# One-token shift ahead of the feed-forward norm: three SBUF-to-SBUF transfers in place of three matmuls

## The chip, the cores and the metric

One core of a Trainium2 chip runs the whole program. The metric is the device time of one execution in microseconds (us).

## What is computed

The input `x` is 16 sequences of 256 tokens of 256 channels. A first block adds cross attention over a short context. The second block works on the normed result: two layers of local attention and a gated feed-forward part. Attention is local, in windows of 128 tokens that also see the window before. A layer is, shortened:

```
h = shift_token(x)                 # second half of the channels: from the token before
q, k, v = split(h @ wqkv)          # l2norm, scale, rotary
x = x + local_attention(q, k, v) @ wo
h = shift_token(x)                 # <- this shift is what is changed
h = (h - mean(h)) / sqrt(var(h) + 1e-5) * lg + lb
a, g = split(h @ w1 + b1)
x = x + (a * gelu(g)) @ w2 + b2
```

`shift_token` keeps channels 0 to 127 and takes channels 128 to 255 from the token before (zeros at the first token).

## The kernel before, in words

All matmuls with weights are made of three products of a high and a low part. The program has a phase for the cross attention (up to about 300 us) and then the layer phase, with which the change deals. There 32 items (2 layers of 16 sequences) go through a software pipeline. Iteration `g` works on four items at once: `a = g` (projection to q, k, v, rotation, turning), `b = g - 1` (scores, softmax, values, output product, first residual), `c = g - 2` (shift, norm, first feed-forward product, gate) and `d = g - 3` (second feed-forward product, second residual). A tile holds a sequence as 2 tiles of 128 tokens on the partitions.

Each engine has its own program in a fixed order written by hand, in a function `run_l(g)`; the engines meet by semaphores. What a step waits for stands in its helper.

- The first residual (VectorE, line 1302) writes `x1[:, :, 0:3:2]`: of the three slots of 128 channels, slot 0 gets the first half and slot 2 the second. Slot 1 is for the second half shifted by one token. Semaphore `dve_x1`.
- TensorE's `shift_down(c)` (lines 678 to 683) waits for `dve_x1` and multiplies slot 2 by a shifted identity: one matmul for tile 0, one for tile 1, and one that brings the last row of tile 0 to the first row of tile 1. It stands between `project(a, d, 0, 1)` and `project(a, d, 0, 0)`. VectorE's `copy_shifted(c)` (line 1307) copies the result to slot 1, and `stats_h(c)` (line 1312) follows, then `rotate(a, 0)` (lines 1350, 1356).
- TensorE's order after that: `feed(c, d, 0)` to `feed(c, d, 5)` (line 788) between projections and scores, `turn_p(..., 0)` (line 748), `turn_h`, `turn_p` 1 and 2, `turn_next` (line 520, transposes of `x_cur` for the next item), `weigh` (line 764), `hidden` 0 to 2, `turn_p(..., 5)`, `weigh`, `hidden` 3 to 5, `out_product`, `turn_qk` (line 826).
- `maxes` (VectorE, line 1371) finds the maxima of a unit of scores; the fifth waits for `turn_p(..., 0)`. `second_residual(d)` (line 1409) waits for the last `feed`, and in layer 2 adds the block's input to it (line 1414). Semaphores `dve_x2` and `dve_out`.
- SyncE issues all transfers, in this order in an iteration: the tail copies (lines 455 and 459: 42 rows of the last chunk of the gated values, copied to further partitions in SBUF, used by `feed(..., 5)`); the load of `x_cur` for item `a + 1` (line 476, needed by `turn_next` of the same iteration, after the wait that the old content has been read); after the wait for `dve_x1` the load of `x_res` for `b` (line 480); after the wait for `dve_x2` or `dve_out` the store of `x2` (line 488); and from item 16 on for `c` the load of `x_orig` (line 490).

Of the kernel before, what the change touches and what calls it, by code (L numbers as in the profile page):

```python
# [25 lines left out]
P = 128  # L26
SEQS, T, D = 16, 256, 256
NT = T // P
# [20 lines left out]
XUNITS = 4  # L49


WEIGHT = {name: n + 1 for n, name in enumerate(
# [26 lines left out]

def identities():  # L80

    return np.eye(P, 2 * P + 4, k=4, dtype=np.float32)


def at(n, per, k):


    if isinstance(n, int):
        return n * per + k
    i, c = n  # L90
    return i * (2 * per) + (c * per + k)
# [20 lines left out]
def build(nc, x, ctx_in, xwq, xwk, xwv, xwo, xbo, wqkv, qsc, ksc, wo, lng, lnb, w1, b1, w2, b2, rope, mask, ident, out):  # L112
    ctx = ExitStack()
    with ctx:
        def sb(name, shape, dt=F32, where=ctx):
            return where.enter_context(nc.sbuf_tensor(name, shape, dt))

        def sem(name):
            return ctx.enter_context(nc.semaphore(name))
# [5 lines left out]
        pb = ctx.enter_context(nc.psum_tensor("pb", [P, 8, 512], F32))  # L125
        ones_at = sb("ones_at", [P, 2 * P + 4])
        id_f, down_f, carry_f = ones_at[:, 4:4 + P], ones_at[:, 3:3 + P], ones_at[:, 3 + P:3 + 2 * P]
        mask_t = sb("mask_t", [P, 2, P])
# [125 lines left out]
            "cur_load", "res_load", "orig_load", "x2_store")]  # L254
        pe_down, dve_down = sem("pe_down"), sem("dve_down")
        pe_xt, act_xhi, dve_xlo = sem("pe_xt"), sem("act_xhi"), sem("dve_xlo")
# [62 lines left out]
        def has_next(a):  # L319
            return a is not None and not (isinstance(a, int) and a == ITEMS - 1)  # L320
# [30 lines left out]
        def _(sp):  # L351
# [111 lines left out]
            sp.wait_ge(y_store, 16 * SEQS)  # L463

            def run_l(g, layer=None):
                a, b, c, d, par = l_roles(g)
                if isinstance(d, int) and d == SEQS:
                    tail_weights(1)
                if isinstance(d, int) and d == 0:
                    sp.wait_ge(zero_made, 2)  # L470
                if d is not None:
                    tail_hi(d)
                    tail_lo(d)
                if has_next(a):
                    sp.wait_ge(pe_xt, at(a, 1, 1))
                    sp.dma_start(x_cur[:], one(y_dram, seq_of(plus(a, 1), layer))).then_inc(cur_load, 16)
                if c is not None:
                    sp.wait_ge(dve_x1, at(c, 1, 1))
                    if b is not None:
                        sp.dma_start(x_res[:], one(y_dram, seq_of(b, layer))).then_inc(res_load, 16)  # L480
                if d is not None:
                    if layer_of(d, layer) == LAYERS - 1:
                        sp.wait_ge(dve_out, at(plus(d, -SEQS), 1, 1))
                        dst = out_rows
                    else:
                        sp.wait_ge(dve_x2, at(d, 1, 1))
                        dst = y_dram
                    sp.dma_start(one(dst, seq_of(d, layer)), x2[:, 1 - par]).then_inc(x2_store, 16)
                    if c is not None and layer_of(c, layer) == LAYERS - 1:
                        sp.dma_start(x_orig[:], one(x1_dram, seq_of(c, layer))).then_inc(orig_load, 16)  # L490

            def between(g):
# [10 lines left out]
        def _(pe):  # L503
# [173 lines left out]

            def shift_down(c):

                pe.wait_ge(dve_x1, at(c, 1, 1))  # L680
                pe.matmul(pb[:, 6, 0:P], down_f, x1[:, 0, 2], start=True, stop=True)
                pe.matmul(pb[:, 6, P:2 * P], down_f, x1[:, 1, 2], start=True, stop=False)
                pe.matmul(pb[:, 6, P:2 * P], carry_f, x1[:, 0, 2], start=False, stop=True).then_inc(pe_down, 1)

            def turn_h(b, c):
# [65 lines left out]
            def weigh(b, c, par, j):  # L751

                pe.wait_ge(act_pt, at(b, UNITS, 2 * j + 2))
                if j == 0:
                    pe.wait_ge(act_v, at(b, NT, NT))
                    if c is not None:
                        pe.wait_ge(dve_down, at(c, 1, 1))
                for k in range(2 if j < 2 else 4):
# [71 lines left out]
            def run_l(g, layer=None):  # L830
# [3 lines left out]
                if a is not None:  # L834
                    project(a, d, 0, 1)
                if c is not None:
                    shift_down(c)
                if a is not None:
# [321 lines left out]
        def _(dve):  # L1160
# [143 lines left out]

            def copy_shifted(c):
                dve.wait_ge(pe_down, at(c, 1, 1))
                nc.vector.tensor_copy(x1[:, :, 1], pb[:, 6, 0:2 * P].rearrange("p (t n) -> p t n", t=NT)).then_inc(dve_down, 1)

            def stats_h(c):
                dve.wait_ge(dve_down, at(c, 1, 1))  # L1310
                for t in range(NT):
                    e = nc.vector.bn_stats(l_st[:, t], x1[:, t, 0:2].rearrange("p c n -> p (c n)"))
                e.then_inc(dve_bst, 1)
                aggregate(l_mv, l_st, dve_bst, dve_bmv, c)
# [107 lines left out]
            def run_l(g, layer=None):  # L1422
# [7 lines left out]
                if c is not None:  # L1430
                    copy_shifted(c)
                    stats_h(c)
# [83 lines left out]
        def _(pool):  # L1516
# [38 lines left out]


            nc.gpsimd.memset(hg_hi[:, FC - 1].bitcast(F32), 0.0).then_inc(zero_made, 1)

# [104 lines left out]
```

## Time and profile before

| | |
|---|---|
| median of 3 runs | 1534.05 us (1534.04 to 1535.44) |
| profiled execution, its own time | 1534.95 us |
| its span, first to last instruction | 1533.1 us |
| TensorE matmuls busy | 1447.2 us (94%) |
| VectorE busy | 1129.9 us (74%) |
| ScalarE busy | 937.8 us (61%) |
| GpSimd busy | 746.9 us (49%) |
| mean granted TensorE clock | 0.98 of full speed |
| share of 16 DMA engines, the queue of all transfers | 11.7% |

The profile shows one execution. PE is TensorE's matmuls, PEld its weight loads, DVE VectorE, ACT ScalarE, POOL GpSimd, and SPq SyncE's sequencer, which issues transfers. Times are us from the start of the span; L520 is line 520. A chain is followed backwards from the last instruction, at each step to what released it. The name behind `<-` in brackets is what ended the idle time before an instruction. The ends of matmuls are modelled, so neighbours overlap in the rows. The granted clock is given as a share of 2.4 GHz: 1.00, or 0.50 for 1.2 GHz.

### The profile page before, as it was taken

Reading aid. Unit: us, or ns where it says so; the run is one execution under the profiler, and the core shown is the slowest. Engines: PE = TensorE matmul, PEld = TensorE weight load, DVE = VectorE, ACT = ScalarE, POOL = GpSimd, SP = SyncE. Lnnn points to the kernel's source line nnn. Section 1 sums busy time; section 2 is a strip of 40 time slices with the busy share of each in tenths; the row PEclk is TensorE's granted clock in tenths of the full one; section 3 lists DMA queues with packets and bytes.
Section 4 is the critical chain, followed back from the end, with each engine's and each line's share of the span. In section 5 each row is a group of like instructions: output and inputs, shape, how many; then the busy total and the mean of one; then the engine's idle time right before and its main releaser. Section 6 shows DMA issues by size and latency. Waiting matters only on the chain.

```text
span 1533.1 us, 33616 instructions
## 1 busy us (share of the span) xinstructions
PE 1447.2 (94%) x11808; PEld 1278.1 (83%) x11808; DVE 1129.9 (74%) x3102; ACT 937.8 (61%) x2670; POOL 746.9 (49%) x570
## 2 busy tenths in 40 slices
PE   4999999868999999999999899999999999999987
PEld 4888888746888888888888788888888888888886
DVE  3766666446788877877777778888788888888874
ACT  2766666435666666666666666666666666666661
POOL 1121121044666666665655555555555655555642
PEclk8999999889999999999999999999999999999999
DMA  6311111200000000000001010011110100001100
GB/s 195 102 55 49 51 54 41 84 29 15 24 24 24 24 24 23 23 23 23 24 26 35 16 56 24 30 39 40 31 31 31 30 30 30 30 30 33 34 24 26
DMA packets 40843, 58.88 MB, mean 38 GB/s; under 512 B 6540, under 2 KB 22448, under 8 KB 40752
## 3 DMA queue, kind: packets, MB, share of 16 engines
q1 hardware_dynamic: 40752, 57.69, 11.7%
q8 instruction: 54, 0.88, 0.2%
q14 instruction: 37, 0.30, 0.1%
HBM read 38.06 MB, written 16.78 MB: 36 GB/s over the span
## 4 chain that ended last, share of the span: by engine, by line
PE 66%; DVE 18%; issue 7%; ACT 4%; POOL 2%; SPq 1%; DMA 1%; DVEq 0%; POOLq 0%; ACTq 0%
PE pb L511 26%; PE pb L788 7%; PE pb L733 6%; PE pb L802 6%; PE pb L764 4%; PE pb L826 4%; DVE p_t L1371 3%; DVE p_t L1385 3%; PE pb L748 3%; DVE r_cos L1350 2%; DVE n_sq L1336 2%; PE pb L572 2%; DVE r_sin L1356 2%; PE pb L560 2%; PE pb L610 2%
## 5 line engine op out<-in xcount | busy, mean ns | idle before, releaser
L1561 POOL TENSOR_TENSOR n_inv<-n_cl,half_neg 128x16 f32<-128x16 f32 x64 | 211.2, 3300 | 199.3 <-DVE n_cl L1341 195.9
L1058 ACT ACTIVATE p_t<-p_t,s_nm 128x128 f32<-128x128 f32 (+1 forms) x512 | 226.6, 444 | 34.5 <-DVE s_nm L1371 31.8
L511 PE MATMUL pb<-h_hi,w_hi 128*128 128x256 f32 x704 | 208.7, 296 | 5.7 <-DVE h_lo L1332 3.3
L511 PE MATMUL pb<-h_hi,w_lo 128*128 128x256 f32 x704 | 199.6, 284 | 0.0
L511 PE MATMUL pb<-h_lo,w_hi 128*128 128x256 f32 x704 | 199.4, 283 | 0.0
L1566 POOL TENSOR_TENSOR r_cos<-r_cos,r_sin 128x1024 f32<-128x1024 f32 x64 | 154.7, 2418 | 89.6 <-DVE r_sin L1356 89.6
L1371 DVE CUSTOM_DVE_ANT_0 p_t<-pb,mask_t 128x128 f32<-128x128 f32 (+1 forms) x512 | 152.0, 353 | 46.3 <-PE pb L733 30.4
L1016 ACT ACTIVATE qk_sq<-pb 128x512 f32<-128x512 f32 x128 | 72.3, 591 | 184.5 <-PE pb L511 184.5
L1049 ACT ACTIVATE pt_t<-pb 128x512 f32<-128x512 f32 x192 | 113.7, 593 | 100.5 <-PE pb L748 100.4
L511 PE MATMUL pb<-wqkv_hi,xt_hi 128*128 128x512 f32 x384 | 166.5, 434 | 5.8 <-DVE r_sin L1356 4.9
L1588 POOL TENSOR_TENSOR hg_lo<-hg,hg_hi 128x256 fp32r<-128x256 f32 x192 | 139.6, 748 | 53.9 <-DVE hg_hi L1402 53.9
L511 PE MATMUL pb<-wqkv_lo,xt_hi 128*128 128x512 f32 x384 | 152.4, 397 | 0.0
L511 PE MATMUL pb<-wqkv_hi,xt_lo 128*128 128x512 f32 x384 | 151.9, 396 | 0.0
L511 PEld LDWEIGHTS pb<-h_hi,w_hi 128*128 128x128 f32 x704 | 134.8, 191 | 17.6 <-issue 6.7
L511 PEld LDWEIGHTS pb<-h_lo,w_hi 128*128 128x128 f32 x704 | 135.3, 192 | 0.0
L511 PEld LDWEIGHTS pb<-h_hi,w_lo 128*128 128x128 f32 x704 | 134.9, 192 | 0.0
L1385 DVE TENSOR_TENSOR p_t<-p_t,s_inv 128x512 f32<-128x512 f32 x192 | 129.4, 688 | 0.1
L748 PE MATMUL pb<-ones_at,p_t 128*128 128x128 f32 x768 | 115.1, 279 | 12.4 <-DVE p_t L1385 11.8
L1573 POOL TENSOR_TENSOR r_cos<-r_cos,n_inv 128x1024 f32<-128x1024 f32 x64 | 122.0, 1906 | 5.0
L1527 POOL TENSOR_TENSOR x_ve<-x_mv,eps_t 128x2 f32<-128x2 f32 x32 | 6.3, 197 | 237.7 <-DVE x_mv L1171 237.0
L733 PE MATMUL pb<-qk_t 64*128 64x128 f32 (+1 forms) x1024 | 111.7, 348 | 5.2 <-DVE wqkv_lo L1164 4.0
L748 PEld LDWEIGHTS pb<-ones_at,p_t 128*128 128x128 f32 x768 | 84.8, 140 | 32.9 <-DVE p_t L1385 19.3
(137 smaller groups left out, 4083.9 us busy)
## 6 DMA issues: line engine op xcount, KB each, us to landing
x_cur<-y_state SPq DMA_DIRECT2D x32, 256.0 KB, 2.7
x_res<-y_state SPq DMA_DIRECT2D x32, 256.0 KB, 2.9
x_in<-x SPq DMA_DIRECT2D x16, 256.0 KB, 2.8
x_state<-x_x SPq DMA_DIRECT2D x16, 256.0 KB, 2.0
y_state<-y_x SPq DMA_DIRECT2D x16, 256.0 KB, 2.1
y_state<-x SPq DMA_DIRECT2D x16, 256.0 KB, 2.0
x_orig<-x_state SPq DMA_DIRECT2D x16, 256.0 KB, 2.8
out<-x SPq DMA_DIRECT2D x16, 256.0 KB, 2.2
```

The costliest lines, as they stand in the source:

```text
L511: mm = pe.matmul(dst, s, m, start=(n == 0 and k == 0), stop=(n == len(pairs) - 1 and k == 2))
L733: mm = pe.matmul(pb[:, S_BANK[u], k * keys:k * keys + keys], qk_t[r:r + DH, 0, ch, q_cols], qk_t[r:r + DH, 1, ch, 0:keys], start=True, sto ...
L748: mm = pe.transpose(pb[:, PT_BANK[u], k * P:k * P + P], p_t[:, u % 4, k * P:k * P + P], id_f)
L788: mm = pe.matmul(pb[:, 7, t * D:t * D + D], s[:, k, rows], m[:, k], start=(k == 0 and j == 0 and t == 0), stop=(k == FC - 1 and t == NT - 1))
L1049: nc.scalar.activation(pt_t[:, u % 4], pb[:, PT_BANK[u]], ACT.Copy).then_inc(act_pt, 1)
L1058: e = nc.scalar.activation(pu, pu, ACT.Exp, bias=s_nm[:, j, k:k + 1], scale=-1.0, accum_out=s_sum[:, j, k:k + 1])
L1371: e = nc.vector.tensor_tensor_reduce(p_t[:, j % 4, k * keys:k * keys + keys], pb[:, S_BANK[j], k * keys:k * keys + keys], m, -1.0, FAR, AL ...
L1385: nc.vector.tensor_tensor(pu, pu, s_inv[:, u, 0:heads].unsqueeze(2).broadcast_to([P, heads, 512 // heads]), ALU.mult).then_inc(dve_pn, 1)
L1561: nc.gpsimd.tensor_tensor(n_inv[:, t], n_cl[:, t], half_neg[:], ALU.pow).then_inc(pool_inv, 1)
L1566: nc.gpsimd.tensor_tensor(r_cos[:, t], r_cos[:, t], r_sin[:, t], ALU.add).then_inc(pool_sum, 1)
L1573: nc.gpsimd.tensor_tensor(rows, rows, n_inv[:, t].unsqueeze(2).broadcast_to([P, 2 * HEADS, DH]), ALU.mult).then_inc(pool_qk, 1)
L1588: nc.gpsimd.tensor_tensor(hg_lo[0:rows, m], hg[0:rows, m], hg_hi[0:rows, m].bitcast(F32), ALU.subtract).then_inc(pool_hglo, 1)
```

## The change

- The three matmuls and the copy are gone, with the shifted parts of the identity constant. Three transfers within SBUF, issued by SyncE, write slot 1 of `x1` from slot 2: rows 0 to 111 to rows 1 to 112 of both tiles, rows 112 to 126 to rows 113 to 127 of both tiles, and row 127 of tile 0 to row 0 of tile 1. The zero row is set once, by GpSimd.
- `stats_h(c)` on VectorE waits for all three.
- SyncE's order in an iteration is now: wait for `dve_x1`, the three shifts, the load of `x_res`; the tail copies; the wait for `dve_x2` or `dve_out`, the store of `x2`, the load of `x_orig`; the load of `x_cur`.
- `weigh(..., 0)` on TensorE, which writes where the shift's result lay, waits for `dve_x1` in place of the copy.

```diff
+SHIFT_PIECES = [(0, 112), (112, 15)]
...
-        pe_down, dve_down = sem("pe_down"), sem("dve_down")
+        shift_load = sem("shift_load")
...
+            def shift_down(c):
+
+                for first, rows in SHIFT_PIECES:
+                    sp.dma_start(x1[first + 1:first + 1 + rows, :, 1], x1[first:first + rows, :, 2]).then_inc(shift_load, 16)
+                sp.dma_start(x1[0:1, 1, 1], x1[P - 1:P, 0, 2]).then_inc(shift_load, 16)
...
-                if isinstance(d, int) and d == 0:
+                if isinstance(g, int) and g == 2:
                     sp.wait_ge(zero_made, 2)
+                if c is not None:
+                    sp.wait_ge(dve_x1, at(c, 1, 1))
+                    shift_down(c)
+                    if b is not None:
+                        sp.dma_start(x_res[:], one(y_dram, seq_of(b, layer))).then_inc(res_load, 16)
                 if d is not None:
                     tail_hi(d)
                     tail_lo(d)
-                if has_next(a):
-                    sp.wait_ge(pe_xt, at(a, 1, 1))
-                    sp.dma_start(x_cur[:], one(y_dram, seq_of(plus(a, 1), layer))).then_inc(cur_load, 16)
-                if c is not None:
-                    sp.wait_ge(dve_x1, at(c, 1, 1))
-                    if b is not None:
-                        sp.dma_start(x_res[:], one(y_dram, seq_of(b, layer))).then_inc(res_load, 16)
-                if d is not None:
                     if layer_of(d, layer) == LAYERS - 1:
                         sp.wait_ge(dve_out, at(plus(d, -SEQS), 1, 1))
...
+                if has_next(a):
+                    sp.wait_ge(pe_xt, at(a, 1, 1))
+                    sp.dma_start(x_cur[:], one(y_dram, seq_of(plus(a, 1), layer))).then_inc(cur_load, 16)
...
-            def shift_down(c):
-
-                pe.wait_ge(dve_x1, at(c, 1, 1))
-                pe.matmul(pb[:, 6, 0:P], down_f, x1[:, 0, 2], start=True, stop=True)
-                pe.matmul(pb[:, 6, P:2 * P], down_f, x1[:, 1, 2], start=True, stop=False)
-                pe.matmul(pb[:, 6, P:2 * P], carry_f, x1[:, 0, 2], start=False, stop=True).then_inc(pe_down, 1)
...
                     if c is not None:
-                        pe.wait_ge(dve_down, at(c, 1, 1))
+                        pe.wait_ge(dve_x1, at(c, 1, 1))
...
-                if c is not None:
-                    shift_down(c)
...
-            def copy_shifted(c):
-                dve.wait_ge(pe_down, at(c, 1, 1))
-                nc.vector.tensor_copy(x1[:, :, 1], pb[:, 6, 0:2 * P].rearrange("p (t n) -> p t n", t=NT)).then_inc(dve_down, 1)
-
             def stats_h(c):
-                dve.wait_ge(dve_down, at(c, 1, 1))
+                dve.wait_ge(shift_load, at(c, 48, 48))
...
+            nc.gpsimd.memset(x1[:, 0, 1], 0.0)
             nc.gpsimd.memset(hg_hi[:, FC - 1].bitcast(F32), 0.0).then_inc(zero_made, 1)
```

## Rows read from the trace of the kernel before

**Rows 1.** The profile's page: TensorE's busy time, and the chain's shares by engine.
```profile
PE 1447.2 (94%) x11808; PEld 1278.1 (83%) x11808; DVE 1129.9 (74%) x3102; ACT 937.8 (61%) x2670; POOL 746.9 (49%) x570
...
PE 66%; DVE 18%; issue 7%; ACT 4%; POOL 2%; SPq 1%; DMA 1%; DVEq 0%; POOLq 0%; ACTq 0%
```

**Rows 2.** Chain in order of time, layer 1: start us, us, engine, line, count.
```profile
645.46 0.66 PE pb L748 x4
...
659.03 0.22 PE pb L681 x2
...
681.91 0.66 PE pb L748 x4
```

**Rows 3.** Chain in order of time, layer 2.
```profile
1167.82 0.66 PE pb L748 x4
...
1204.73 0.66 PE pb L748 x4
```

**Rows 4.** TensorE timeline, layer 1: start us, us, engine, line, op [idle before].
```profile
671.58 0.39 PE L788 MATMUL pb<-w_hi,hg_hi 128*128 128x256 f32 x2
...
674.53 0.60 PE L520 MATMUL pb<-ones_at,x_cur 128*128 128x128 f32 x4
...
681.91 0.66 PE L748 MATMUL pb<-ones_at,p_t 128*128 128x128 f32 x4 [0.22 <-DVE p_t L1385]
```

**Rows 5.** VectorE timeline, layer 1.
```profile
656.57 0.69 DVE L1302 TENSOR_TENSOR x<-pb,x_res 128x512 f32<-128x512 f32 x1 [1.18 <-PE pb L802]
...
660.20 0.75 DVE L1312 BATCH_NORM_STATS2 l_st<-x 128x6 f32<-128x256 f32 x2
...
662.32 1.29 DVE L1350 TENSOR_TENSOR r_cos<-pb,cos_t 128x512 f32<-128x512 f32 x2 [0.84 <-ACT qk_sq L1016]
...
670.55 0.29 DVE L1371 CUSTOM_DVE_ANT_0 p_t<-pb,mask_t 128x128 f32<-128x128 f32 x1 [0.52 <-PE pb L748]
...
672.11 0.69 DVE L1409 TENSOR_TENSOR x<-pb,x1b 128x512 f32<-128x512 f32 x1
```

**Rows 6.** SyncE timeline, layer 1 (issues of transfers).
```profile
657.72 0.34 SPq L476 DMA_DIRECT2D x_cur<-y_state  x1
...
672.98 0.36 SPq L488 DMA_DIRECT2D y_state<-x  x1
```

**Rows 7.** Issues of the tail copy: duration ns min/median/max, first and last start us.
```profile
L459 SPq DMA_DIRECT2D hg_hi<-hg_lo x32: 745/746/752, 401.2 to 1526.4; - x32
```

**Rows 8.** Timeline, end of the run: the last tail copy and who waited.
```profile
1526.37 0.75 SPq L459 DMA_DIRECT2D hg_hi<-hg_lo  x1
...
1528.60 0.47 PE L788 MATMUL pb<-w_hi,hg_hi 128*128 128x256 f32 x2 [1.87 <-DMA hg_hi<-hg_lo]
```

**Rows 9.** Transfers by line (last: median us to landing); x_cur's landings.
```profile
x_res<-y_state SPq DMA_DIRECT2D x32, 256.0 KB, 2.9
...
DMA to landing us min/median/max: 2.5/2.7/4.9
```

**Rows 10.** Timeline, layer 2: VectorE, SyncE and TensorE around the last addition.
```profile
1195.42 0.69 DVE L1414 TENSOR_TENSOR x<-x,x_orig 128x512 f32<-128x512 f32 x1 [0.25 <-DVE x L1409]
...
1196.28 0.41 SPq L488 DMA_DIRECT2D out<-x  x1
...
1196.89 0.33 SPq L490 DMA_DIRECT2D x_orig<-x_state  x1
1196.90 0.60 PE L520 MATMUL pb<-ones_at,x_cur 128*128 128x128 f32 x4
```

**Rows 11.** Windows: length, busy of PE, PEld, DVE, ACT, POOL, granted clock, DMA.
```profile
1512.00:1516.50 4.50, 4.04 (x21) 4.08 (x22) 1.09 (x3) 0.47 (x1) 0.00 (x0) 0.62 0.21 58
1509.20:1512.40 3.20, 0.00 (x0) 0.00 (x0) 2.97 (x4) 1.02 (x2) 1.70 (x1) 1.00 0.38 108
...
313.00:316.00 3.00, 3.00 (x14) 2.44 (x13) 2.11 (x2) 0.84 (x2) 2.89 (x2) 1.00 0.02 6
```

**Rows 12.** TensorE timeline, layer 1's first iteration.
```profile
312.68 0.50 PE L511 MATMUL pb<-wqkv_hi,xt_hi 128*128 128x512 f32 x1 [2.36 <-DVE r_sin L1356]
```

More of the change, by code:

```diff
@@ L77, in masks, with identity @@
     return np.stack([np.where(j < i, MASKED, 0.0), np.where(j > i, MASKED, 0.0)], 1).astype(np.float32)
-def identities():
-    return np.eye(P, 2 * P + 4, k=4, dtype=np.float32)
+def identity():
+    return np.eye(P, dtype=np.float32)
 def at(n, per, k):
@@ L125, in build @@
         pb = ctx.enter_context(nc.psum_tensor("pb", [P, 8, 512], F32))
-        ones_at = sb("ones_at", [P, 2 * P + 4])
-        id_f, down_f, carry_f = ones_at[:, 4:4 + P], ones_at[:, 3:3 + P], ones_at[:, 3 + P:3 + 2 * P]
+        ones_at = sb("ones_at", [P, P])
+        id_f = ones_at[:]
         mask_t = sb("mask_t", [P, 2, P])
@@ L1430, in run_l @@
                 if c is not None:
-                    copy_shifted(c)
                     stats_h(c)
@@ L1651 @@
         "w2": w2, "b2": np.asarray(L0_ffn_b2),
-        "rope": rope_tables(), "mask": masks(), "ident": identities(),
+        "rope": rope_tables(), "mask": masks(), "ident": identity(),
     }
```

## The prediction

> **What bounds the kernel now.** I read the page's busy shares and its chain first: TensorE is busy 94% of the span and carries 66% of the chain [rows 1]. Then the chain in order of time. In the first feed-forward layer it runs through TensorE without a gap across the start of each iteration, the three shift matmuls among it (two passes and 0.22 us each, 0.66 us in all), up to the scores of the third pair; from there through VectorE (maxima, rotation, squares, probabilities), and back to TensorE at `turn_p(5)` [rows 2]. `turn_p(5)` recurs every 36.45 us in layer 1 (645.46 to 681.91) and every 36.91 us in layer 2 [rows 2, 3]. The TensorE timeline shows how little room there is: its one idle time in a layer-1 iteration is 0.22 us before `turn_p(5)` [rows 4]. So TensorE sets the pace with VectorE just behind it, and whatever makes TensorE wait for a transfer is added to every iteration. Last I read the SyncE timeline [rows 6], because the change rewrites that queue.
>
> **Removed.** The matmuls: 3 x 0.22 = 0.66 us of the path [rows 2]. The VectorE copy out of PSUM and its wait for them go too; what follows the copy starts at 660.20 [rows 5].
>
> **Added: three transfers, and a wait for them on VectorE.** The residual ends at 656.57 + 0.69 = 657.26 [rows 5]. SyncE follows a VectorE end by 0.18 us (672.11 + 0.69 = 672.80, issue at 672.98) [rows 5, 6], so the first shift is issued at 657.44. The trace shows no such transfer. The nearest is the SBUF-to-SBUF tail copy, whose issue takes 0.75 us [rows 7]; a load from DRAM takes 0.34 [rows 6]. I take 0.75, and guess 0.05 us between: the third is issued at 657.44 + 2 x 0.80 = 659.04. The run's last tail copy was issued at 1526.37 and the matmul that waited for it began at 1528.60: 2.2 us [rows 8]. So `stats_h` starts at 661.3. Between 660.20 and the rotation at 662.32 VectorE has 1.28 us of work and 0.84 us of waiting for ScalarE [rows 5]; that wait covers most of the delay of 1.1 us, and the rotation starts 661.3 + 1.28 - 662.32 = 0.26 us later. VectorE now comes to the fifth maxima at 670.03 and waits 0.52 us for TensorE, until 670.55 [rows 5]. After the change it comes at 670.29, and TensorE would let it go at 670.55 - 0.66 = 669.89. So `second_residual` ends 0.26 us earlier, not 0.66: the wait costs d = 0.4 us. Queued behind it on VectorE are `rotate(a, 0)`, for which `project(a, 1, 0)` waits on TensorE, the next maxima, and `norm_probs`; all are passed on with the same 0.26 us at most.
> Bounds of d: with issues of 0.34 us, as for DRAM, the third piece is issued at 658.22 and there at 660.4, and d = 0; with a landing of 2.9 us [rows 9] d = 1.1. I take 0.4, since its rows are of the same kind of transfer.
> The Trainium skill, "DMA: Bandwidth & Descriptors", section "Issuing engines are not separate DMA queues", says that the time a sequencer takes to initiate a transfer is usually small beside the transfer. The tail copy disagrees (0.75 of 2.2 us). By the rule d would be 0 and the time some 11 us lower.
>
> **Moved: the tail copies and `x_res`.** The tail copies go behind the shifts and the `x_res` load, to about 661, and land by 664; `feed(5)` uses them at 671.58 [rows 4]. Cover 7 us: no cost; without it they would stall TensorE. `x_res` is loaded some 2 us later and used in the next iteration: no cost. The memory set on GpSimd and the smaller table of constants are there once: nothing.
>
> **Moved: the load of `x_cur`.** This is the costly part. It goes behind the wait for `dve_x2` (`dve_out` in layer 2), the store of `x2` and, from g = 18, the load of `x_orig`; but `turn_next` needs it in the same iteration. Today it is issued 17 us ahead (657.72, used at 674.53) [rows 4, 6].
> Layer 1: `second_residual` ends at 672.80, `turn_x` begins at 674.53, 1.73 us later. After the change the store is issued at +0.18, `x_cur` 0.6 later (as 1196.28 to 1196.89 [rows 10]), at about +0.76. The second of two transfers in a row lands 2.9 us after its issue (`x_res` [rows 9]), so TensorE starts at +3.7. The stall is 3.66 - 1.73 = 1.93, with d 2.33 us. It swallows the 0.22 us of idle time, and 0.66 us of work are gone: +1.45 us per iteration.
> Layer 2: the last addition ends at 1195.42 + 0.69 = 1196.11, `turn_x` begins at 1196.90, 0.79 us later [rows 10]. After: store at +0.17, `x_orig` at +0.78, `x_cur` at +1.33, landed at +4.23, matmul at +4.28 [rows 9, 10]. Stall 3.49 + 0.4 = 3.9 us. From `turn_x` to `turn_p(5)` are 7.83 us here and 7.38 in layer 1 [rows 3, 4, 10], so 0.45 + 0.22 = 0.67 us of waits are swallowed: 3.89 - 0.67 - 0.66 = +2.56 us.
> The Trainium skill, same page, section "Rules for kernel authors", says to issue a transfer early, compute, and wait for it late. It speaks against this part of the change, and the 17 us of lead in the trace agree with it.
>
> **The clock.** From 1509.2 to 1512.4 TensorE did nothing; from 1512.0 to 1516.5 its granted clock was 0.62 on average, which is 0.38 / 0.5 x 4.5 = 3.4 us at the half level (1.2 GHz) [rows 11]. An idle time of 2.36 us in layer 1's first iteration was followed by full clock, 1.00 from 313 to 316 [rows 11, 12]. So the 3.9 us of layer 2 should drop it and the 2.3 us of layer 1 should not. Price: 3.4 us at half speed lose 1.7 us.
>
> **The sum.** There is a late `x_cur` load for g = 3 to 30. g = 3 to 17: 15 x 1.45 = 21.8. g = 18 (store, `x_orig`, `x_cur`, no second addition): 2.1. g = 19 to 30: 12 x 2.56 = 30.7, and for the clock 12 x 1.7 = 20.4. Four iterations have a shift and no such load: -1.5. Together +73.5 us, worked out from a profiled execution of 1534.95 (span 1533.1 and 1.85 around it). It lies 0.9 above the median of 1534.05, from which I count: 1607.
>
> **Rivals.**
> (A) The load is late, but the clock holds in layer 2. For it: a stall between two dense stretches is not quite the one case that the trace shows. Against: that case was shorter than 3.9 us and lost the clock. 1587; with d = 0 also 1576 (15 x 1.05 + 1.7 + 12 x 2.16 - 2 = +41).
> (B) The clock falls in layer 1 too. For it: 2.3 us is at the edge of what the rows show to be harmless, and d may be larger. 16 x 1.7 = 27: 1634, and 1650 with d near 1.
> (C) Faster: the load comes in time, so that only the matmuls' 0.66 us (0.26 with d) count. It decides at a landing 1.73 - 0.76 = 0.97 us after issue or sooner; then 32 x 0.66 = 21 gives 1513, 32 x 0.26 = 8 gives 1526. Against: the fastest `x_cur` landing of the trace took 2.5 us [rows 9]. For it is only that I may have misread the order of the queue.
> (D) The wait on VectorE costs more than the matmuls did: third piece later than 661.6, d above 0.66. With d = 1.1, 28 x 0.7 = 20 more: 1627.
>
> **How the numbers follow.** Forecast 50%, A 20%, B 14%, D 9%, C 4%, others 3%. The range takes in A with d = 0 and B: 1577 to 1636. A measurement of this kernel can tell about 0.2% (3 us) from no change; by the cases: faster 0.04, same 0.02, slower 0.94.
>
> **What would show it.** Right: TensorE waits at line 520's matmul for the DMA of `x_cur`, 2.3 us in layer 1 and near 4 in layer 2; granted clock 0.5 behind it in layer 2 alone; `turn_p(5)` every 37.9 and about 41 us; the wait ahead of BATCH_NORM_STATS2 ends some 4 us after the residual. Wrong: no wait there, shift issues of 0.35 us, or a clock of 1.00 throughout.

## The result, and the profile after

| | before | after |
|---|---|---|
| median | 1534.05 us (3 runs) | 1583.86 us (4 runs, 1578.82 to 1592.75) |
| profiled execution | 1534.95 us | 1582.53 us |
| its span | 1533.1 us | 1580.5 us |
| TensorE matmuls busy | 94% | 91% |
| mean granted clock | 0.980 | 0.969 |

The kernel became slower: the ratio is 1.033, 95% interval 1.029 to 1.037. The forecast was 1607, its range 1577 to 1636. Direction and place were as forecast: the late load of `x_cur` is the loss. The cost was 50 us by the medians (47 between the two profiled spans, which are taken apart below), and not 73. One execution of all runs below is left out: one of the four of "The load ahead of the store" took 4746.57 us, three times the others.

The page of after: span, TensorE's busy time with fewer instructions than before, and the chain's shares by engine and by line. They answer to [rows 1].

```profile
span 1580.5 us, 33304 instructions
...
PE 1434.9 (91%) x11616; PEld 1268.4 (80%) x11616; DVE 1106.3 (70%) x3070; ACT 939.3 (59%) x2670; POOL 745.3 (47%) x571
...
PE 72%; DVE 10%; DMA 7%; issue 3%; SPq 3%; ACT 3%; POOL 2%; DVEq 0%; POOLq 0%; ACTq 0%
PE pb L518 32%; PE pb L788 6%; PE pb L764 6%; PE pb L733 6%; PE pb L802 5%; DMA x_cur<-y_state 5%; PE pb L748 4%; PE pb L826 4%; PE pb L579 2%; PE pb L567 2%; PE pb L617 2%; DVE p_t L1365 2%; PE pb L621 2%; DVE p_t L1379 2%; DVE x L1403 1%
```

PE is TensorE's matmuls, DVE VectorE, SPq SyncE's issues of transfers. TensorE is busy 12.3 us less than before, and transfers carry 7% of the chain (1% before). One kind of transfer, the load of `x_cur`, carries 5%. The sums of waits from 400 to 1480 us (who waits, for what: us in all, times, longest) say who sits idle for it:

```profile
PE pb L527 <- DMA x_cur<-y_state: 62.2, 28, 4.3
...
DVE l_st L1306 <- DMA x<-x: 46.9, 27, 4.4
```

TensorE lost 62.2 us in 28 waits at line 527 (line 520 before), where it waited for no transfer before. The 46.9 us at line 1306 are VectorE's wait for the shifts. The two look alike in size, and only the chain tells that they are not alike in cost. The chain of after in order of time (start us, us, what), in layer 1 and in layer 2:

```profile
601.01 0.70 DVE x L1403
...
612.08 0.44 PE pb L748 x4
...
638.72 0.38 SPq L492
...
639.36 2.68 DMA x_cur<-y_state
...
642.09 0.66 PE pb L527 x4
...
649.08 0.44 PE pb L748 x4
```
```profile
1225.02 2.84 DMA x_cur<-y_state
...
1227.90 0.66 PE pb L527 x4
```

Second residual (line 1403), store of `x2` (638.72), load of `x_cur` (639.36, 2.68 us), transposes of it (642.09): the chain of [rows 2, 3] now runs through these transfers, once in each of the 28 iterations that have the late load. `turn_p(5)` (612.08, 649.08) recurs every 37.00 us, against 36.45 in [rows 2]. The shifts stand in the chain of these 1080 us at three places only, 402.79, 887.92 and 1008.50, none of them in the regular iterations.

VectorE, SyncE and TensorE in the same iteration (start us, us, engine, line, operation, in brackets the idle time before); they answer to [rows 4 to 6]:

```profile
622.82 0.69 DVE L1300 TENSOR_TENSOR x<-pb,x_res 128x512 f32<-128x512 f32 x1 [1.04 <-PE pb L802]
...
626.94 0.75 DVE L1306 BATCH_NORM_STATS2 l_st<-x 128x6 f32<-128x256 f32 x2 [1.41 <-DMA x<-x]
...
628.07 1.29 DVE L1344 TENSOR_TENSOR r_cos<-pb,cos_t 128x512 f32<-128x512 f32 x2
...
636.30 0.29 DVE L1365 CUSTOM_DVE_ANT_0 p_t<-pb,mask_t 128x128 f32<-128x128 f32 x1 [0.53 <-PE pb L748]
...
637.85 0.69 DVE L1403 TENSOR_TENSOR x<-pb,x1b 128x512 f32<-128x512 f32 x1
```
```profile
623.54 1.65 SPq L469 DMA_DIRECT2D x<-x  x2
625.24 0.60 SPq L470 DMA_DIRECT2D x<-x  x1
626.03 0.43 SPq L482 DMA_DIRECT2D x_res<-y_state  x1
...
638.72 0.38 SPq L492 DMA_DIRECT2D y_state<-x  x1
639.36 0.34 SPq L497 DMA_DIRECT2D x_cur<-y_state  x1
```
```profile
642.09 0.66 PE L527 MATMUL pb<-ones_at,x_cur 128*128 128x128 f32 x4 [1.65 <-DMA x_cur<-y_state]
```

The three shifts take SyncE 1.65 + 0.60 us to issue, `stats_h` starts at 626.94 and the rotation at 628.07; at 636.30 VectorE still waits 0.53 us for TensorE, as it did in [rows 5]. So the wait for the shifts is absorbed in layer 1 before it reaches TensorE. The wait for `x_cur`, 1.65 us, is not.

In layer 2 the same wait is longer, and behind some waits the clock falls. TensorE's waits, and windows of 8 us behind the start of `turn_x` (length, busy of PE, PEld, DVE, ACT, POOL with counts, granted clock, share of DMA, GB/s):

```profile
1189.29 0.66 PE L527 MATMUL pb<-ones_at,x_cur 128*128 128x128 f32 x4 [2.92 <-DMA x_cur<-y_state]
...
1227.90 0.66 PE L527 MATMUL pb<-ones_at,x_cur 128*128 128x128 f32 x4 [3.22 <-DMA x_cur<-y_state]
```
```profile
1189.00:1197.00 8.00, 7.71 (x74) 7.20 (x76) 5.56 (x9) 4.73 (x11) 7.81 (x4) 1.00 0.00 1
1228.00:1236.00 8.00, 8.00 (x62) 7.50 (x63) 4.80 (x7) 2.88 (x6) 7.81 (x4) 0.79 0.00 0
1065.00:1073.00 8.00, 7.45 (x47) 6.82 (x48) 4.92 (x7) 2.03 (x8) 7.74 (x4) 0.59 0.01 3
1107.00:1115.00 8.00, 8.00 (x55) 7.34 (x54) 4.43 (x7) 2.16 (x4) 7.81 (x4) 0.66 0.00 0
1149.00:1157.00 8.00, 8.00 (x58) 7.34 (x58) 3.74 (x5) 2.34 (x5) 7.81 (x5) 0.72 0.01 2
642.00:650.00 8.00, 7.91 (x78) 7.41 (x80) 6.46 (x10) 5.78 (x15) 7.81 (x4) 1.00 0.00 0
```

Clock 1.00 behind the wait of 2.92 us, 0.79 behind that of 3.22, and 0.59, 0.66 and 0.72 near 1065, 1107 and 1149. A mean of 0.79 over 8 us is 0.21 / 0.5 x 8 = 3.4 us at the half level (1.2 GHz), 0.59 is 6.6 us; near 1107 and 1149 the fall begins before the window, while TensorE still waits. In layer 1 it stays at 1.00.

Where the 47.4 us of the span came from, by the starts of `turn_x`:

| stretch | before | after | more |
|---|---|---|---|
| to the first iteration with a late load | 419.18 | 420.29 | 1.1 |
| 12 periods of layer 1 | 36.5 each | 36.9 each | 5.4 |
| 4 periods around the change of layer | 156.4 | 162.4 | 6.1 |
| 11 periods of layer 2 | 36.8 each | 39.7 each | 32.6 |
| from there to the end | 115.2 | 117.5 | 2.2 |

### The profile page after: what moved, and what is told of

Same layout as the page of the kernel before. It is cut to its first block, busy times and chain, and to the rows that moved or that the text cites. A ratio compares the mean times of both kernels' runs of the same rounds, so it can differ in the third digit from the quotient of the medians.

```text
span 1580.5 us, 33304 instructions
## 1 busy us (share of the span) xinstructions
PE 1434.9 (91%) x11616; PEld 1268.4 (80%) x11616; DVE 1106.3 (70%) x3070; ACT 939.3 (59%) x2670; POOL 745.3 (47%) x571
## 4 chain that ended last, share of the span: by engine, by line
PE 72%; DVE 10%; DMA 7%; issue 3%; SPq 3%; ACT 3%; POOL 2%; DVEq 0%; POOLq 0%; ACTq 0%
PE pb L518 32%; PE pb L788 6%; PE pb L764 6%; PE pb L733 6%; PE pb L802 5%; DMA x_cur<-y_state 5%; PE pb L748 4%; PE pb L826 4%; PE pb L579 2%; PE pb L567 2%; PE pb L617 2%; DVE p_t L1365 2%; PE pb L621 2%; DVE p_t L1379 2%; DVE x L1403 1%
## 5 line engine op out<-in xcount | busy, mean ns | idle before, releaser
L1365 DVE CUSTOM_DVE_ANT_0 p_t<-pb,mask_t 128x128 f32<-128x128 f32 (+1 forms) x512 | 152.2, 353 | 38.5 <-PE pb L733 27.0
L1389 DVE SCALAR_TENSOR_TENSOR hg<-pb,b_t,gl 128x256 f32<-128x256 f32 x192 | 86.3, 477 | 85.4 <-ACT gl L1035 65.4
L518 PEld LDWEIGHTS pb<-h_hi,w_hi 128*128 128x128 f32 x704 | 138.0, 196 | 9.4 <-issue 6.2
```

Of the source, the lines that this page charges most:

```text
L518: mm = pe.matmul(dst, s, m, start=(n == 0 and k == 0), stop=(n == len(pairs) - 1 and k == 2))
L1365: e = nc.vector.tensor_tensor_reduce(p_t[:, j % 4, k * keys:k * keys + keys], pb[:, S_BANK[j], k * keys:k * keys + keys], m, -1.0, FAR, AL ...
```

## The experiments

The theory was: all of the loss is the late load of `x_cur`, the stall itself in both layers and the clock in layer 2. The rivals: the wait for the shifts costs something of its own; the clock has no part in it; what the shift gains hangs on how its rows are cut. The period quoted is the time from one `turn_x` to the next.

### The shift alone, with the load early

Everything of the change, but the load of `x_cur` is issued right behind that of `x_res`.

```diff
                     if b is not None:
                         sp.dma_start(x_res[:], ...).then_inc(res_load, 16)
+                if has_next(a):
+                    sp.wait_ge(pe_xt, at(a, 1, 1))
+                    sp.dma_start(x_cur[:], ...).then_inc(cur_load, 16)
                 if d is not None:
                     tail_hi(d)
...
-                if has_next(a):
-                    sp.wait_ge(pe_xt, at(a, 1, 1))
-                    sp.dma_start(x_cur[:], ...).then_inc(cur_load, 16)
```

> The changed kernel with one thing undone: the load of `x_cur` stands right behind that of `x_res` again, ahead of the wait for `dve_x2`. Theory (the late load is all of the loss, and the three shifts cost nothing): TensorE no longer waits at the transposes of `x_cur`, an iteration takes 36.45 - 0.66 = 35.8 us in layer 1, the clock stays at 1.00 behind them, and the time is 1534 - 21 = 1513 us, up to 1517 since the shift of g = 16 lands late behind a weight load. Rival 1 (the wait for the shifts costs d = 0.4 us as forecast): 1526. Rival 2 (the transfers cost more than the matmuls did, whatever the load does): over 1534.

Measured: 1522.6 us, ratio 0.992 (0.991 to 0.994), faster than before. The period is 35.80 us in layer 1, 0.65 less than before: the three matmuls' 0.66 us are a gain in full, so d is 0. VectorE's timeline of this kernel shows the wait for the shifts, and behind it the wait for TensorE at the fifth maxima:

```profile
614.34 0.69 DVE L1300 TENSOR_TENSOR x<-pb,x_res 128x512 f32<-128x512 f32 x1 [1.04 <-PE pb L802]
...
618.45 0.75 DVE L1306 BATCH_NORM_STATS2 l_st<-x 128x6 f32<-128x256 f32 x2 [1.39 <-DMA x<-x]
...
627.82 0.29 DVE L1365 CUSTOM_DVE_ANT_0 p_t<-pb,mask_t 128x128 f32<-128x128 f32 x1 [0.53 <-PE pb L748]
```

`stats_h` waits 1.39 us and starts 3.42 us behind the end of the residual, and at 627.82 VectorE still has 0.53 us to spare. TensorE's waits for `x_cur` are gone. The whole loss of the change is in the place of the load. The total is 5 to 10 us above what was expected; the periods were as expected, and the difference lies at three places outside the loop, taken up with the last experiment.

### The late load alone

The kernel before with its matmuls, only the load of `x_cur` moved.

```diff
-                if has_next(a):
-                    sp.wait_ge(pe_xt, at(a, 1, 1))
-                    sp.dma_start(x_cur[:], ...).then_inc(cur_load, 16)
                 if c is not None:
...
                         sp.dma_start(x_orig[:], ...).then_inc(orig_load, 16)
+                if has_next(a):
+                    sp.wait_ge(pe_xt, at(a, 1, 1))
+                    sp.dma_start(x_cur[:], ...).then_inc(cur_load, 16)
```

> The kernel before with the three matmuls and the copy, and only the load of `x_cur` moved behind the store of `x2` and the load of `x_orig`. Theory (late load alone, and it adds to the matmuls): the loss of the changed kernel plus the 0.66 us that it saves, 1584 + 21 = 1605 us; layer 1 takes 37.0 + 0.66 = 37.7 us an iteration. Rival (the late load costs only because the shifts delay VectorE and so `second_residual`): under 1570.

Measured: 1597.14 us, ratio 1.041 (1.040 to 1.043). TensorE's timeline, one wait of each layer:

```profile
644.72 0.66 PE L520 MATMUL pb<-ones_at,x_cur 128*128 128x128 f32 x4 [1.53 <-DMA x_cur<-y_state]
```
```profile
1155.91 0.66 PE L520 MATMUL pb<-ones_at,x_cur 128*128 128x128 f32 x4 [3.52 <-DMA x_cur<-y_state]
```

Without any shift transfer the load costs 63 us, and the rival (under 1570) is out. The two parts add up: -12 for the shift (the experiment before) and +63 for the load make +51, against the +50 of the whole change.

### The load ahead of the store

The load of `x_cur` still behind the wait for `dve_x2` or `dve_out`, but before the store and the load of `x_orig`. That takes two issues of SyncE from its way (in layer 1 one) and leaves the wait for VectorE.

```diff
                         sp.wait_ge(dve_out, at(plus(d, -SEQS), 1, 1))
...
+                    if has_next(a):
+                        sp.dma_start(x_cur[:], ...).then_inc(cur_load, 16)
                     sp.dma_start(one(dst, seq_of(d, layer)), x2[:, 1 - par]).then_inc(x2_store, 16)
...
-                if has_next(a):
+                if d is None and has_next(a):
```

> The changed kernel with the load of `x_cur` still behind the wait for `dve_x2` or `dve_out`, but ahead of the store of `x2` and of the load of `x_orig` (its wait for the transposes of the iteration before is left out, since `dve_x2` comes after them). It is issued 0.64 us sooner in layer 1 and 1.21 in layer 2. Theory (the stall is issue time plus landing, so it shrinks by just that, and below some 2 us it keeps the clock): stalls of 1.0 us in layer 1 and 1.8 in layer 2, no window of low clock behind them, 1584 - 15 x 0.64 - 12 x 1.2 - about 16 for the clock = 1544 us. Rival (the stall is set by transfers that share the engines, or the clock falls for another reason): stalls stay near 1.6 and 3.0 us, 1570 or more.

Measured: 1551.21 us (three executions, 1550.07 to 1552.04), ratio 1.011 (1.009 to 1.013). SyncE and TensorE in layer 2:

```profile
1204.10 0.35 SPq L493 DMA_DIRECT2D x_cur<-y_state  x1
1204.65 0.42 SPq L494 DMA_DIRECT2D out<-x  x1
1205.26 0.34 SPq L496 DMA_DIRECT2D x_orig<-x_state  x1
```
```profile
1206.91 0.66 PE L529 MATMUL pb<-ones_at,x_cur 128*128 128x128 f32 x4 [1.94 <-DMA x_cur<-y_state]
```

The load now leads the two other issues, which put it 1.2 us later in the changed kernel (1225.02 in its chain, with the store at 1223.79), and the wait falls from about 3 to 1.94 us. In layer 1 it falls by some 0.4. The stalls account for about 15 x 0.4 + 12 x 1.1 = 19 us of the 33 that the edit wins; the rest goes with most of the drops of the clock: the period of layer 2 is 37.2 to 37.5 us, and in three iterations 38.6 to 38.9. In these three the granted clock is 0.79, 0.79 and 0.81 (windows of 8 us from 1017, 1131 and 1357), behind waits of only 1.86, 2.05 and 2.07 us, while it stays at 1.00 behind one of 2.13 (1244.41). So "below some 2 us it keeps the clock" did not hold. The forecast of 1544 had left out those three, some 1.4 us each, and had the stall of layer 1 shrink by 0.64 us.

### The stall filled

To tell the clock from the stall: in layer 2's loop TensorE makes 16 transposes of the identity, which nobody reads, just before it waits for `x_cur`. The loop holds iterations 22 to 29, so 8 of the 12 full stalls of layer 2 are filled, from the one near 1144 us on. If the clock has no part in it, nothing is gained.

```diff
+                if c is not None and layer == 1:
+                    for k in range(16):
+                        pe.transpose(pb[:, 3, (k % 4) * P:(k % 4) * P + P], id_f, id_f)
                 turn_x(plus(a, 1))
```

> The changed kernel with 16 transposes of the identity (about 1.8 us of TensorE work that nobody reads) ahead of the transposes of `x_cur` in layer 2's loop, inside the stall of 3 us. Theory (the low clock behind the stall costs about 18 us by itself): the clock stays at 1.00 in the loop of layer 2, every iteration of it takes 38.6 us in place of 38.6 or 39.95 in turn, and the time falls to about 1570 us although TensorE does more. Rival (the low clock costs nothing since the rest of the iteration has room): 1584. Rival (the work lengthens the path): over 1590.

Measured: 1574.67 us, ratio 1.027 (1.025 to 1.028), 9 us less than the change. TensorE's idle time before `turn_x` falls to 2.5 us in the first filled iteration and 1.2 to 1.4 in the seven behind it. Windows of 8 us behind `turn_x`, of the same columns as above:

```profile
1184.00:1192.00 8.00, 8.00 (x82) 7.49 (x84) 5.50 (x8) 4.67 (x10) 7.81 (x4) 1.00 0.01 3
1223.00:1231.00 8.00, 8.00 (x87) 7.66 (x88) 4.91 (x7) 4.79 (x8) 7.81 (x4) 1.00 0.00 0
```

Behind the first filled wait (2.47 us) the clock still falls, 0.79 from 1144 to 1152, and that period is 39.95 us. The next six periods are 38.34 to 38.57 us, with no low clock in them. In after they were 38.6 where the clock stayed at 1.00 and 39.9 where it fell. So a drop costs 1.3 to 1.4 us, and the stall alone 38.5 - 36.1 = 2.4 us in layer 2. Of the 8 us between the two profiled executions the filled iterations make up some 4 (309.9 us from the `turn_x` near 1144 to the last one, 314.1 in after). The others lie ahead of them, mostly in unfilled iterations of layer 2 where the clock also fell for less time, so they are not the filler's.

### The shift in four and in five pieces

Both have the load early. If the wait for the shifts has a little room in layer 1, one issue more should use it up and a second one cost its time. (`stats_h` waits for the number of pieces.)

```diff
-SHIFT_PIECES = [(0, 112), (112, 15)]
+SHIFT_PIECES = [(0, 64), (64, 48), (112, 15)]
```

> The kernel with the early load (1522.6 us), its shift cut into four transfers (rows 64, 48, 15 and the one between tiles), so the last is issued 0.82 us later. Theory (VectorE waits 0.53 us for TensorE at the fifth maxima, and only a delay beyond that counts): 0.82 - 0.53 = 0.3 us late there, an iteration of 36.0 to 36.1 us in layer 1 in place of 35.80, and 1530 to 1533 us in all. Rival 1 (the delay counts in full): 1548. Rival 2 (there is more cover than 0.53, for instance the 0.23 us of idle time of TensorE further on): 1524.

```diff
-SHIFT_PIECES = [(0, 112), (112, 15)]
+SHIFT_PIECES = [(0, 32), (32, 32), (64, 48), (112, 15)]
```

> The same with five transfers (32, 32, 48, 15 rows and the one), the last issued 1.65 us later than with three. Theory: 1.65 - 0.53 = 1.1 us late at the fifth maxima, an iteration of 36.8 to 36.9 us in layer 1, and 1522.6 + 32 x 1.1 = 1558 us. Rival 1 (in full): 1575. Rival 2 (more cover): under 1550.

Measured: 1532.82 us, ratio 0.999 (0.998 to 1.000), and 1549.84 us, 1.010 (1.009 to 1.012). The periods of layer 1 are 35.9 and 36.5 us. VectorE in the two kernels:

```profile
661.20 0.75 DVE L1306 BATCH_NORM_STATS2 l_st<-x 128x6 f32<-128x256 f32 x2 [2.23 <-DMA x<-x]
```
```profile
624.92 0.69 DVE L1300 TENSOR_TENSOR x<-pb,x_res 128x512 f32<-128x512 f32 x1 [1.04 <-PE pb L802]
...
630.35 0.75 DVE L1306 BATCH_NORM_STATS2 l_st<-x 128x6 f32<-128x256 f32 x2 [2.72 <-DMA x<-x]
```

`stats_h` starts 4.15 us behind the residual in the first and 630.35 - 625.61 = 4.74 in the second (3.42 with three pieces). 0.7 us later costs 0.1 us per iteration, 1.3 later 0.7. So the slack of the shift in this kernel ends near 4.1 us, and with three pieces 0.6 us of it is left. I had expected 1558 of the second: its pieces of 32 rows take SyncE only 0.6 to 0.7 us to issue, where the sum had 0.82. The first came out at the expected 1530 to 1533, but by two errors: its regular period is 35.9 us and not 36.0 to 36.1, and the late iterations of the next paragraph make up for it.

In both kernels about every eighth iteration takes 0.8 to 1.7 us more, with `stats_h` as late as 6.0 us behind the residual (517.58 in the first of them). In the first of them three such iterations make up about 4.5 of the 10 us that it loses to the kernel with three pieces. At the same places one issue of SyncE takes 1.3 to 1.5 us in place of some 0.4 (515.49, 840.20 and 1108.98), and a transfer of the queue that the profile calls `instruction` stands within 0.4 us of each (515.4, 839.9 and 1108.6). That suggests that SyncE waited for its own program; as such transfers also stand where nothing is late, it is not shown.

### One transfer of 127 rows

```diff
-SHIFT_PIECES = [(0, 112), (112, 15)]
+SHIFT_PIECES = [(0, 127)]
```

> The kernel with the early load, its 127 rows of both tiles shifted by one transfer, and the row between tiles by a second. Theory (the rows go over all engines): one issue less, and the same 1522 us or slightly less. Rival (all rows go through one DMA engine): at a sixteenth of the 350 GB/s that a 256 KB load reaches here 127 KB take 5.9 us or more, the statistics start some 8 us after the residual in place of 3.4, VectorE is 4 us late, an iteration takes near 40 us, 1522.6 + 32 x 4 = 1650 us. The Trainium skill, 'DMA: Bandwidth & Descriptors', section 'Why a DMA increments its semaphore by 16 and not by 1', says that a transfer is split over the largest number of engines up to 16 that divides its rows, which for 127 is one: it speaks for the rival.

Measured: 1758.53 us, ratio 1.145 (1.144 to 1.147). One transfer less to issue, and the worst kernel of all. SyncE, VectorE and TensorE:

```profile
623.52 0.74 SPq L469 DMA_DIRECT2D x<-x  x1
624.31 4.91 SPq L470 DMA_DIRECT2D x<-x  x1
```
```profile
622.80 0.69 DVE L1300 TENSOR_TENSOR x<-pb,x_res 128x512 f32<-128x512 f32 x1 [1.19 <-PE pb L802]
...
633.23 0.75 DVE L1306 BATCH_NORM_STATS2 l_st<-x 128x6 f32<-128x256 f32 x2 [7.82 <-DMA x<-x]
```
```profile
636.83 0.79 PE L518 MATMUL pb<-wqkv_hi,xt_hi 128*128 128x512 f32 x1 [5.37 <-DVE r_sin L1350]
```

The data are there 9.7 us behind the residual, with 127 KB moved; 112 KB in a piece of 112 rows take 2.3 us from their issue. VectorE waits 7.8 us and TensorE 5.4, and the mean granted clock of the run is 0.926 (0.981 with the early load and three pieces), so part of the loss is the clock's. And SyncE itself is held up: the next issue takes 4.91 us where that of one row takes 0.60 else. The rival of 1650 had the direction, not the size (it had neither the clock nor that issue in it). The Trainium skill, "DMA: Bandwidth & Descriptors", section "Why a DMA increments its semaphore by 16 and not by 1", says that the number of DMA engines is the largest number up to 16 that divides the outermost size, so that 127 rows go through one engine. The trace agrees: from 626 to 629 us the mean busy share of the 16 engines is 0.07, and one of 16 would be 0.0625; the rows do not show the engines one by one. The cut at 112 + 15 rows avoids this.

### The shifts behind the loads

The three shifts behind `x_res` and `x_cur`, to see whether transfers of 512 KB ahead of them delay them by more than the issues.

```diff
-                    shift_down(c)
                     if b is not None:
                         sp.dma_start(x_res[:], ...).then_inc(res_load, 16)
...
+                if c is not None:
+                    shift_down(c)
```

> The kernel with the early load, but the three shifts behind the loads of `x_res` and `x_cur` in SyncE's queue, and so issued 1.15 us later. Theory A (only issue time counts): the last shift is issued 1.15 us later, 0.6 us late at the fifth maxima, 1522.6 + 20 = 1542 us. Theory B (the shift's data also queue behind 512 KB of loads, as at g = 16 where it lands 6 us after issue behind a weight load): landing 3 us or more in place of 1.7, 2 us late, 1585 us.

Measured: 1547.43 us, ratio 1.009 (1.007 to 1.010); the period of layer 1 is 36.3 us. The page's lines of this transfer (KB each, median us to landing), first of the kernel with the shifts first, then of this one:

```profile
x<-x SPq DMA_DIRECT2D x32, 112.0 KB, 2.3
```
```profile
x<-x SPq DMA_DIRECT2D x32, 112.0 KB, 2.8
```

The 112 rows land 0.5 us later behind the loads, the 15 rows 0.3 and the single row, which is the last, less than 0.1 (1.75 against 1.71). So what the place costs in a regular iteration is SyncE's time of issue (theory A), and theory B is out. The 25 us in all are more than A's 20, because four single iterations (among them that of the weight load) are 1.8 to 4.1 us longer than with the shifts first, where the regular ones are 0.2 to 0.9 longer.

### A version that beats both

The early load, and at the change of layer two heavy transfers moved from ahead of the shift to behind it: the load of the second layer's `w1` (1408 KB, at g = 16) to behind the store, and the copy of the weights' tail (at g = 19) behind the shift.

```diff
-                if isinstance(d, int) and d == SEQS:
-                    tail_weights(1)
...
                     tail_lo(d)
+                    if isinstance(d, int) and d == SEQS:
+                        tail_weights(1)
...
+                    if isinstance(g, int) and g == SEQS:
+                        sp.wait_ge(w_lo, WEIGHT["qkv1"])
+                        load_w1(1)
...
-                    sp.wait_ge(w_lo, WEIGHT["qkv1"])
-                    load_w1(1)
```

> The kernel with the early load of `x_cur`, and the two weight transfers that stand ahead of the shift once each (the load of the second layer's w1 at g = 16, the copy of the tail weights with its wait at g = 19) moved behind it. Theory (the early-load kernel saves 12 us in place of 21 since the shift is late in a few single iterations: 0.6 us at g = 16, 2.9 at g = 19, 3 in the last two, where VectorE has nothing else to do): the first two come back, 1522.6 - 3.5 = 1519 us. Rival (the iterations at the layers' boundary are late for another reason): 1522.6.

Measured: 1520.51 us, ratio 0.991 (0.990 to 0.992): 13.5 us or 0.9% faster than before. What the shift had met at these two places, at g = 16 in after and at g = 19 in the kernel with the early load:

```profile
893.99 0.75 DVE L1306 BATCH_NORM_STATS2 l_st<-x 128x6 f32<-128x256 f32 x2 [4.41 <-DMA x<-x]
```
```profile
986.28 0.77 SPq L452 DMA_DIRECT2D w_hi<-w_lo  x1
...
987.10 2.01 SPq L469 DMA_DIRECT2D x<-x  x2
...
990.92 0.75 DVE L1306 BATCH_NORM_STATS2 l_st<-x 128x6 f32<-128x256 f32 x2 [3.29 <-DMA x<-x]
```

VectorE waited 4.41 us for a shift that stood behind the weights, and at g = 19 the shift was issued only behind the tail copy (986.28), which itself waits for a split of weights that ends at 986.25, so that `stats_h` came 990.92 - 984.58 = 6.3 us after the residual. The period at g = 19 fell from 40.10 to 36.53 us and that at g = 16 from 43.22 to 41.62. Of these 5.2 us only 2 show in the median, and those are not clear of the noise: the intervals of the two ratios, 0.991 to 0.994 with the early load alone and 0.990 to 0.992 here, overlap. In the profiled execution the first iterations ran 3.3 us later than before the edit (`turn_x` at 384.09 against 380.78). There the clock was lower: 0.85 on average from 330 to 380 us, against 1.00 in the kernel with the early load.

## Why the prediction was right, and where its sizes were off

The direction and the path (SyncE's queue, the late `x_cur`, TensorE's wait) were right. The size came inside the range at its lower end, 7 us above 1577, and in part by a wide range: that bound belonged to a clock that holds with d = 0, and of these two only d = 0 came true.

**What bounds it, and the removed matmuls.** Right: with the load early the period falls by 0.65 us against the 0.66 of the matmuls.

**The wait for the shifts (d = 0.4).** The measured d is 0. `stats_h` starts at 626.94, 3.43 us behind the residual's end, where the sum had 661.3 - 657.26 = 4.04. The landing was the mis-sized term: 1.7 us from the issue of the single row (625.24) to the start, where I had taken the 2.2 of a copy of 42 rows [rows 8]. The issues were near what [rows 7] gave (1.70 us from the first to the third, for 1.60), and the first began 0.03 us behind the residual, not 0.18. The work from there to the rotation takes 1.13 us, not 1.28. By the experiment with four pieces even 4.04 us would have cost under 0.1 us: the room behind the rotation was larger than one comparison of ready times let me see.
The rule of the Trainium skill, "DMA: Bandwidth & Descriptors", section "Issuing engines are not separate DMA queues", that the issue is usually small beside the transfer gave d = 0, which came true, but not by its reason: issuing the 112 rows takes 0.70 of 2.3 us.

**The late load in layer 1 (+1.45 per iteration).** `x_cur` reaches TensorE 3.55 us behind `second_residual` (638.54 to 642.09; 3.66 forecast), and TensorE is ready 1.90 us behind it (1.73 forecast). That makes a stall of 1.65 and not 2.33, d being gone. Measured per period: +0.45. The stall costs 36.95 - 35.80 = 1.15 us of its 1.65, since waits that stood elsewhere are swallowed, 0.5 us of them and not 0.22. That could have been read beforehand from starts in place of idle times. From `turn_x` to the `weigh` behind `turn_p(5)` it is 682.49 - 674.53 = 7.96 us before and 649.45 - 642.09 = 7.36 after:

```profile
682.49 1.97 PE L764 MATMUL pb<-pt_t,v_t 128*64 128x128 f32 x32
```
```profile
649.45 1.97 PE L764 MATMUL pb<-pt_t,v_t 128*64 128x128 f32 x32
```

The row's idle time of 0.22 us is too small for what the wait cost, since the ends of matmuls are modelled and overlap: they last 0.28 us in the rows and start every 0.12. By starts the wait of `turn_p(5)` cost 0.38 us, and 0.2 more come back at two groups of transposes on this stretch. By starts the stall is 1.8 us, too: the transposes ahead of `turn_x` start 2.68 us before it, and 0.87 where it does not wait. 1.8 - 0.6 is the 1.2 us that a period grows by.

**The late load in layer 2 (+2.56).** The stall was forecast as 3.9 and is 2.9 to 3.2 us. Without d it would have been 3.5; the rest is that TensorE comes later and that the load lands in 2.73 to 2.84 us, not 2.9. It costs 38.55 - 36.11 = 2.44 us per period where the clock holds (36.11 with the early load). Less the matmuls this is 1.7 to 1.8 us for the +2.56.

**The clock (12 x 1.7 = 20.4).** Right in kind: the late load brings drops in layer 2 and none in layer 1. Wrong in price and in the rule behind it. The clock fell behind 8 of the 12 full stalls of layer 2: near 1026, 1066, 1107 and 1149, and then behind every second one (1228, 1306, 1385, 1463). A drop of 3.4 us costs 1.37 us, and not 1.7. Of the 32.6 us of the 11 periods some 13 are what they take above 38.55 us each, and so the clock's with all that follows from it.

The step that failed is the one that took a single case, 3.2 us of idle time, for a rule for every longer wait, and one of 2.36 us for a sign that shorter ones are harmless. In after, waits of 2.92 to 3.00 us kept the clock (1189, 1267, 1346 and 1424 us) and of 3.17 to 3.22 lost it (1228, 1306 and 1385), but 2.82 (1463), 2.90 (1026), 2.89 (1066) and 3.03 (1107) lost it too, and three of the first four drops lasted 6.8 us. With the late load alone a wait of 2.33 us (992) lost it and one of 3.26 (1237) kept it, and with the load ahead of the store 1.86 was enough. Even the harmless case turns over: the same 2.36 us of [rows 12] are there in after, ahead of 312.39, and the clock from 314 to 317 is 0.50. So no length in these runs separates the two, and what decides is open. That the stalls of layer 1 (1.2 to 1.8 us) never lost it is what the runs show, and not a rule. The four runs of after differ by 14 us, and the longer ones have the lower mean clock (0.971 at 1578.8, 0.960 at 1592.8).

**What was left out.** The load of `w1` ahead of the shift at g = 16 and the tail copy of the weights ahead of it at g = 19 are on the queue that I read, and are among the +6.1 us of the change of layer. The last iteration, too: there no projection covers the wait for the shifts, and the end of the run with an early load is 2.9 us longer than before (118.1 against 115.2 us from the last `turn_x`). This is why the early load gained 12 us and not 21: my rival C with d = 0 (1513) counted 32 iterations alike.

**The sum.** The forecast had 73.5 us. Too large were d (27 x 0.4 = 10.8), the stalls without it (15 x 0.28 + 12 x 0.45 = 9.6), what is swallowed in layer 1, which was taken as too little (15 x 0.28 = 4.2) and the clock (20.4 - 13 = 7.4). That takes the sum to 41.5; the 6 us up to 47.4 are about what was left out. The sum's -1.5 for the four iterations without a late load has no working: by its own terms it is 4 x 0.26 = 1.0 with d, or 4 x 0.66 = 2.6 without. Rival A, the clock holding, is refuted by the windows; its 1587 lies so near to the result only because the other terms were too large.

## What to carry to other kernels

When an edit brings a new transfer into a queue, look first at what is pushed behind it, and where that is needed: here the transfers that the change is about gain 12 us and a load moved past one wait costs 63. The move was not needed for the shift, so it can be undone and the gain kept. And one row in which the clock falls is no threshold: in these runs stalls from 1.9 to 3.3 us went both ways, so give the clock a range of its own and not all or nothing.

## What the hardware showed beyond this

- A copy within SBUF takes SyncE 0.70 us to issue for 112 rows and 0.90 for 15 (the rows above show the two together, 1.65), 0.60 for one row and 0.6 to 0.7 for 32, against mostly 0.34 to 0.43 for a load of `x_cur` or `x_res` from DRAM. It lands 2.3 us after the start of its issue (112 rows, 112 KB), 2.1 (15 rows) and 1.7 (one row).
- 127 rows in one transfer need 4 times the time of 112 (9.7 against 2.3 us), and SyncE's next issue takes 4.3 us longer (4.7 to 8.3 us in all 32 iterations): there a slow transfer held up the sequencer that issued it, and not only those who waited for its data.
- Behind 512 KB of loads a shift lands up to 0.5 us later; behind 1408 KB of weights (g = 16) it landed after 5.4 to 6.0 us.
- The granted clock fell to the half level behind waits of TensorE for `x_cur` from 1.86 us on, and stayed at 1.00 behind others of up to 3.26; a drop inside layer 2 lasted 3.4 or 6.8 us.
